# Two weight units loaded and split ahead of the first batch, with the head of an adaLN transformer block reordered

## The reference

```python
mod = (_silu(c) @ wmod).reshape(4, 6, 1, 256)           # sa, ca, ga, sb, cb, gb
h = _layernorm(x) * (1 + ca) + sa                        # x: (4, 512, 256)
x = x + ga * attention(h)                                # 16 heads of 16, causal
h = _layernorm(x) * (1 + cb) + sb
x = x + gb * (shared_ffn(h) + top1_of_8_experts(h))      # inner size 512
```

## Time and profile before

| | |
|---|---|
| median of 3 runs | 450.55 us (447.5 to 451.66) |
| the profiled execution | 449.91 us, of which 448.2 us span |
| granted TensorE clock, mean | 0.983 of full speed |
| PE / DVE / ACT / POOL busy | 89 / 70 / 51 / 48% of the span |
| head (to the first unit of transposed scores) | 0 to 51.2 us |
| block of batch 0 | 51.2 to 105.3 us |

### The profile page before, as it was taken

How to read it: one execution, slowest core, us unless ns; L and a number is a source line. 1 busy time by engine, 2 the same in 40 slices (tenths; PEclk the granted TensorE clock), 3 DMA queues, 4 the chain that set the end, 5 groups by cost and what they waited for, 6 DMA issues and landing times.

```text
span 448.2 us, 8602 instructions
## 1 busy us (share of the span) xinstructions
PE 398.8 (89%) x3009; PEld 225.9 (50%) x3009; DVE 315.2 (70%) x635; ACT 227.8 (51%) x408; POOL 213.1 (48%) x251
## 2 busy tenths in 40 slices
PE   3989987999998997969988799999989999999991
PEld 3344544345453463524444355575566666666660
DVE  7788598689989898699959854979734344443441
ACT  2626557886667865367865655362313332333320
POOL 4755955542376824475536743101602655546242
PEclk9989999999999999899999899999999999999997
DMA  8665499669835599343347014991811344343210
GB/s 272 188 153 118 169 230 252 202 226 308 239 104 174 156 272 283 126 129 114 98 148 231 1 48 173 395 352 66 226 58 26 79 81 96 68 83 70 27 21 0
DMA packets 46192, 67.96 MB, mean 152 GB/s; under 512 B 5380, under 2 KB 33668, under 8 KB 46152
## 3 DMA queue, kind: packets, MB, share of 16 engines
q1 hardware_dynamic: 31064, 36.74, 28.3%
q10 hardware_dynamic: 9936, 22.55, 15.1%
q0 software_dynamic: 5152, 8.14, 9.3%
HBM read 43.14 MB, written 25.18 MB: 152 GB/s over the span
## 4 chain that ended last, share of the span: by engine, by line
PE 60%; DVE 21%; ACT 7%; issue 4%; DMA 3%; POOL 3%; ACTq 1%; SPq 0%; DVEq 0%; POOLq 0%
PE bank L1521 38%; DVE mx L1153 6%; PE bank L1677 4%; PE bank L1661 4%; PE bank L1632 2%; DVE rowg L1254 2%; PE bank L1901 2%; ACT W L903 2%; PE bank L1609 2%; DVE W L1254 1%; DVE x_sb L1198 1%; PE bank L1536 1%; DMA stage<-in_wmod 1%; PE bank L1602 1%; PE bank L1859 1%
## 5 line engine op out<-in xcount | busy, mean ns | idle before, releaser
L903 ACT ACTIVATE W<-bank 128x512 f32<-128x512 f32 (+1 forms) x176 | 93.6, 561 | 55.1 <-PE bank L1661 36.8
L1153 DVE TENSOR_REDUCE mx<-bank 128x1 f32<-128x384 f32 (+3 forms) x176 | 104.7, 632 | 18.4 <-PE bank L1634 15.7
L1521 PE MATMUL bank<-W 128*128 128x256 f16 (+2 forms) x756 | 104.2, 290 | 4.5 <-DVE x_sb L1198 1.8
L1521 PEld LDWEIGHTS bank<-W 128*128 128x128 f16 x756 | 72.8, 99 | 37.4 <-issue 7.3
L770 POOL TENSOR_SCALAR_AFFINE_SELECT W<-W 128x512 f32<-128x512 f32 x64 | 47.9, 749 | 81.8 <-ACT W L903 81.8
L1661 PE MATMUL bank<-W 128*128 128x512 f16 (+3 forms) x256 | 63.2, 304 | 12.1 <-ACT W L903 10.1
L1521 PE MATMUL bank<-W,h2T 128*128 x276 | 67.1, 380 | 0.8 <-issue 0.8
L846 POOL DMA_INDIRECT out<-h2T,sidx x23 | 36.3, 1578 | 63.9 <-DVE h2T L1491 63.5
L1632 PE MATMUL bank<-W 126*128 126x128 f16 (+3 forms) x208 | 52.5, 303 | 5.3 <-DVE mx L1153 4.5
L1677 PE MATMUL bank<-W 128*32 128x128 f32 (+3 forms) x512 | 48.5, 453 | 0.8 <-POOL W L770 0.8
L1661 PEld LDWEIGHTS bank<-W 128*128 128x128 f16 x256 | 21.3, 98 | 48.7 <-ACT W L903 29.5
(11 more groups left out here) (172 smaller groups left out, 562.8 us busy)
## 6 DMA issues: line engine op xcount, KB each, us to landing
w_d<-rowg ACTq DMA_DIRECT2D x18, 512.0 KB, 3.8
W<-w_d SPq DMA_DIRECT2D x18, 512.0 KB, 8.1
stage<-in_gup ACTq DMA_DIRECT2D x14, 512.0 KB
qk_d<-W SPq DMA_DIRECT2D x48, 128.0 KB
W<-qk_d SPq DMA_DIRECT2D x32, 192.0 KB, 5.4
stage<-in_down ACTq DMA_DIRECT2D x7, 512.0 KB
x_sb<-in_x SPq DMA_DIRECT2D x4, 512.0 KB, 8.9
h_d<-gbb SPq DMA_DIRECT2D x4, 512.0 KB, 4.6
```

Source lines behind the costliest of these rows:

```text
L903: a.activation(PT[j][:, i:i + m, :], t_bank(N)[:, 0:m * w].rearrange("p (i n) -> p i n", i=m), ACT.Exp).then_inc(s_exp, 1)
L1153: v.tensor_reduce(mx_v[:, b % 2, hp0 // 4, par, i:i + m, t], s_bank(N)[:, 0:m * w].rearrange("p (i n) -> p i n", i=m), AX.X, ALU.max).then ...
L1521: i = t_.matmul(outp, l, r, start=(n == 0), stop=(n == len(prods) - 1), **kw)
```

## The change

Five edits. **1.** `wmod` is laid out by column blocks, one block in each slot of `stage`, so that slot k comes free with the k-th product that reads it. **2.** SP starts the loads of the units 0 and 1 ahead of its first `qk_out`, and that of unit 2 ahead of the first `maxima_out`. **3.** The units 0 and 1 are split in the head (ACT at n = 14 and 17, DVE at n = 39 and 42) and moved at the steps 1 and 3 of block 0; the other units of block 0 are spread over its steps anew, 6 in place of 8. **4.** `norm1(1)` goes from DVE to ACT, as one activation with a scale and a bias; POOL makes the bias (`shift1`, two small operations). **5.** `stats1(1)` goes from before the head's maxima to n = 17, and the first "v" from n = 13 to n = 11.

```diff
@@ -98,20 +98,33 @@
-          0: {6: 0, 12: 1, 18: 2, 23: 3, 28: 4, 33: 5, 38: 6, 43: 7},
+          0: {6: 2, 13: 3, 20: 4, 26: 5, 33: 6, 40: 7},
...
+HIGHS1, LOWS1, MOVES1 = {14: 0, 17: 1}, {39: 0, 42: 1}, {45: 0, 47: 1}
...
+def low_at(n):
+
+    return LOWS1[n + BU] if n + BU in LOWS1 else splits_at(n - LOWS)
+
+
+def moved_at(n):
+
+    return MOVES1[n + BU] if n + BU in MOVES1 else splits_at(n - MOVES)
...
-HEAD = [(13, "v", 0, 0), (17, "v", 0, 1), (24, "turn", 1, 0), (24, "turn", 1, 1), (20, "mod", 0, 1),
+HEAD = [(11, "v", 0, 0), (17, "v", 0, 1), (24, "turn", 1, 0), (24, "turn", 1, 1), (20, "mod", 0, 1),
@@ -273,7 +287,7 @@
-        wm = stage[:, :, :].rearrange("p a b -> p (a b)").rearrange("p (k n) -> p k n", k=KC)
+        wm = [stage[:, c].rearrange("p (k n) -> p k n", k=KC) for c in range(3)]
@@ -577,7 +592,9 @@
             def stage_load(k):
                 if k == 0:
-                    sp.wait_ge(s_mp, 2)
+                    sp.wait_ge(s_mc, 1)
+                else:
+                    sp.wait_ge(s_mp, k)
                 unit_in(sp, k)
@@ -591,19 +608,19 @@
+            stage_load(0)
+            stage_load(1)
             qk_out(0, 0)
             stacks(0, 0)
             qk_out(0, 1)
             stacks(0, 1)
+            stage_load(2)
             maxima_out(0, 0)
             maxima(0, 0)
-            stage_load(0)
-            stage_load(1)
             qk_out(1, 0)
...
             stacks(1, 0)
-            stage_load(2)
@@ -717,6 +734,13 @@
+            def shift1(b):
+
+                c = slice(TT * b, TT * (b + 1))
+                po.wait_ge(s_rstd, b + 1)
+                link(g.tensor_tensor(mr1[:, :], mv1[:, c, 0], rs1[:, c], ALU.mult))
+                g.tensor_scalar(mr1[:, :], mr1[:, :], -1.0, 0.0, ALU.mult, ALU.add).then_inc(s_shift, 1)
@@ -794,9 +818,10 @@
-            rstd(ve1, mv1, rs1, 1, s_mv, s_rstd)
             qk_low(0, 2)
             qk_low(0, 3)
+            rstd(ve1, mv1, rs1, 1, s_mv, s_rstd)
+            shift1(1)
@@ -893,6 +918,16 @@
+            def norm1(b):
+
+                ac.wait_ge(s_rstd, b + 1)
+                ac.wait_ge(s_shift, 1)
+                ac.wait_ge(s_xt, KC * b)
+                for t in range(TT):
+                    n = TT * b + t
+                    a.activation(xn[:, t], x_sb[:, n], ACT.Identity, bias=mr1[:, t:t + 1],
+                                 scale=rs1[:, n:n + 1]).then_inc(s_xn, 1)
@@ -996,6 +1031,7 @@
             query_parity(1)
+            norm1(1)
@@ -1024,9 +1060,11 @@
+                    if b < 0 and n in HIGHS1:
+                        split_high(HIGHS1[n])
                     if n in SPLITS[b]:
                         split_high(SPLITS[b][n])
-                    moved = splits_at(BU * b + n - MOVES)
+                    moved = moved_at(BU * b + n)
@@ -1328,7 +1366,6 @@
-            stats1(1)
@@ -1336,8 +1373,8 @@
-                    if b < 0 and n == 19:
-                        norm1(1)
+                    if b < 0 and n == 17:
+                        stats1(1)
@@ -1371,7 +1408,7 @@
-                    low = splits_at(BU * b + n - LOWS)
+                    low = low_at(BU * b + n)
```

More of the change, by code:

```diff
@@ L197, in build @@
         rs1 = sb("rs1", [P, NT])
+        mr1 = sb("mr1", [P, TT])
         st2 = sb("st2", [P, NT, 6])
@@ L338, in build @@
         s_rstd = sem("s_rstd")
+        s_shift = sem("s_shift")
         s_xn = sem("s_xn")
@@ L520, in _ @@
             wmod_v = wmod.rearrange("(k p) n -> p k n", p=P)
-            sp.dma_start(wm[:, :, 0:2 * H], wmod_v[:, :, 0:2 * H]).then_inc(s_wm, 16)
+            sp.dma_start(wm[0], wmod_v[:, :, 0:2 * H]).then_inc(s_wm, 16)
             sp.dma_start(bqk[:, :], bqkc).then_inc(s_bqk, 16)
             sp.dma_start(wq_s, wqkvT.rearrange("(k p) n -> p k n", p=P)).then_inc(s_wq, 16)
-            sp.dma_start(wm[:, :, 2 * H:4 * H], wmod_v[:, :, 2 * H:4 * H]).then_inc(s_wmr[0], 16)
-            sp.dma_start(wm[:, :, 4 * H:6 * H], wmod_v[:, :, 4 * H:6 * H]).then_inc(s_wmr[1], 16)
+            sp.dma_start(wm[1], wmod_v[:, :, 2 * H:4 * H]).then_inc(s_wmr[0], 16)
+            sp.dma_start(wm[2], wmod_v[:, :, 4 * H:6 * H]).then_inc(s_wmr[1], 16)
             sp.dma_start(bvb, bqkv[2 * H:3 * H].partition_broadcast(P)).then_inc(s_bias, 16)
@@ L1528, in modulation_columns @@
                     for k in range(KC):
-                        i = t_.matmul(T2[:, 4 * c:4 * c + 4], wm[:, k, P * c:P * (c + 1)], cs[:, 1, k],
+                        i = t_.matmul(T2[:, 4 * c:4 * c + 4], wm[0][:, k, P * c:P * (c + 1)], cs[:, 1, k],
                                       start=(k == 0), stop=(k == KC - 1))
@@ L1535, in modulation_rows @@
                 for k in range(KC):
-                    i = t_.matmul(side_bank("mod", 0, c)[0:B, :], cs[:, 1, k], wm[:, k, 512 * (c + 1):512 * (c + 2)],
+                    i = t_.matmul(side_bank("mod", 0, c)[0:B, :], cs[:, 1, k], wm[c + 1][:, k],
                                   start=(k == 0), stop=(k == KC - 1))
```

## The result

| | median | runs |
|---|---|---|
| before | 449.16 us (447.5 to 451.66) | 4 |
| changed | 453.76 us (451.85 to 455.07) | 4 |

The ratio is 1.0096, with a 95% interval from 1.0056 to 1.0137: 4.3 us slower, where 2.2 us faster was forecast. The profiled execution took 454.18 us, of which 452.4 us span.

What follows compares the result with a forecast made beforehand. Bound taken as PE in most of the head, ACT and PE to 56 us, DVE to 68.5, PE from 77 to 105. 2.0 - 0.3 - 0.1 + 0.3 + 0.3 = 2.2 us off 450.55: 448.4 us, range 445.3 to 451.3.

Steps and rivals of the forecast that it cites:

- The head: Ahead of block 0: without PE's 1.91 us pause behind the first scores, a gain of 2.0 us, bounds 1.2 and 2.2.
- Low halves in the head: Two DVE low halves before block 0: free on DVE, may slow POOL; cost 0.3 us, bounds 0 and 1.6.
- Start of block 0: Moves behind exponentials 1 and 3 may leave ACT idle: cost 0.1 us, bounds 0 and 0.8.
- The keys: Keys of batch 1 through memory, 51 to 63 us: no term in the sum; delay counted only in the slower rival.
- slower rival: Moves 0 and 1 delay batch 1's keys 5.6 us: 452.3 us, chance 0.09; decides from a delay of some 4.5 us.
- signs of being wrong: ACT at modulation rows after 36, PE's key wait at step eleven over 3 us, or 105 us gain not kept.
- Rest of block 0: Fewer, wider-spaced high and low halves shrink PE's later waits: gain 0.3 us, bounds a loss of 0.7, a gain of 1.7.
- The wait of 0.71 at 99.95: PE's wait for ACT in block 0, from a move at step 37 and high half at 38; it goes.
- The 0.98 at 85.12: PE's wait for ACT, from the high half at step 23 with the projections; it moves to the next units.
- The trip of the maxima: Negated maxima through memory before step 22: earlier traffic shortens PE's 0.80 us wait; gain 0.3 us, at most 1.5.
- What is won or lost by 105 us reaches the end: Behind 105 us nothing is tied to a fixed time, so what is won by then should reach the end whole.

Runs made afterwards that it cites:

- e2: Changed kernel with the transfers of moves 0 and 1 cut to one partition each, all places in the lists kept; ratio 0.9956 to the kernel before.
- e5: Changed kernel with only the stores of moves 0 and 1 cut to one partition, their loads whole; ratio 1.0005 to the kernel before.
- e6: Changed kernel with only the loads of units 3 and 4 cut to one partition, the stores whole; ratio 0.9987 to the kernel before.
- e7: e4 with the high halves of block 0 at steps 18, 21, 30, 35, 40, 43; ratio 0.9975 to the kernel before.
- e9: Changed kernel with the low halves of units 2 to 7 cut to 128x64; ratio 1.0057 to the kernel before.
- e4: Changed kernel with moves 0 and 1 back at steps 10 and 16, units 2 to 7 respaced; ratio 0.9957 to the kernel before.
- e10: Kernel before with the low halves of units 2 to 7 cut to 128x64; ratio 0.9971 to the kernel before uncut.

## Why the prediction was wrong

**The head (2.0, measured 1.44).** The mechanism was right at each row: pause gone, the "v" at 1.48 us, the clock at 1.00 behind it, `norm1` on ACT from 31.20 (forecast 30.8), `h_parts` from 35.56 (35.4). The pair of `shift1` took 0.2 us each, less than the 0.6 for both; the four activations took 2.08 and not 1.71. Of the 1.93 us at the group behind the second "v" 0.5 went by 42 us; 0.20 of it is PE waiting at 35.70 for ACT's copy, the place that the prediction named. The size was off by 0.6, inside its bounds.

**Low halves in the head (-0.3).** They did slow POOL: two low halves of its projections (L775) took 3.25 us where they took 2.27, and the last of the keys left at 49.77 behind them. e2 has the same low halves in the head and PE waits 0.69 us for the keys, so without the bytes it costs nothing; what it adds to the wait beside them wasn't measured apart.

**Start of block 0 (-0.1).** Right: ACT idled 0.67 us, PE 0.17.

**The keys (0, measured -4.8).** This is the step that failed. The prediction wrote of its slower rival "1.8 us remain, and these are covered", and left the keys out of the sum; the chance was 0.09. One of its own signs of being wrong, a wait of PE for keys by more than 3 us, is what came (5.18). The traffic was counted against the whole ten microseconds from 50 to 60 and found to fit. But the keys don't use the mean of ten microseconds: they pass through twice, the last piece out from 50.4 to 57.0 and back from 58.9 to 66.5, while transfers were busy 0.89 of the time from 51 to 55 and 1.00 from 55 to 60, and e5 and e6 show that half of the bytes already cost 1.6 to 1.8 us. The rival's own working was good: "5.6 us late", a loss of 4 us in all, and 452.3 us, 1.5 below the measured 453.76. It was given "a delay of some 4.5 us on" as its condition; 4.8 was measured. What was held against it, that reads and writes are spread over all queues, did not keep the keys clear of the moves. By the Trainium skill (DMA: Bandwidth & Descriptors, "Issuing engines are not separate DMA queues") transfers started by different engines interleave on the same 16 DMA engines. The runs agree: ACT's moves made the wait for SP's keys 5.18 and not 0.69 us. The prediction quoted this rule and then gave it too little weight, as no row of the kernel before showed it.

**Rest of block 0 (+0.3, measured -1.26 between steps 22 and 44).** The wait of 0.71 at 99.95 went as forecast. The 0.98 at 85.12 was read wrongly: the prediction gave it to the high half at step 23, but 0.97 remains at the same unit with that high half at 26, and with it at 21 in e7, and 0.67 came at the unit behind. What cost most is the wait of 1.56 for POOL. The prediction priced the spread of high halves on ACT alone; the low half follows two steps later on DVE, and one came to lie on POOL's residual bias (e9). The loss passed the bound of "a loss of 0.7" by 0.56 us, and what the bound left out is the 0.98 us that POOL lost, a price that the row of 1.42 for 0.64 had already shown, and that the prediction used for the head only.

**The trip of the maxima (+0.3).** It did get shorter: issue to issue 2.1 us (72.13 to 74.22) where it was 3.5, and the 0.80 of the earlier trace rows is gone; transfers were busy 0.67 of the time from 66 to 72, before 0.80. Between the keys and step 22 the pauses of PE that its timeline lists fell from 3.0 to 0.5 us. But the rest of that stretch took 12.4 us at the lower clock, where e2, with the same list and the clock at 1.00, took 10.5. In all 0.87 us of the keys' loss came back: 3.37 us late at the keys, 2.50 at step 22. The lower clock, some 1.9 us, stood nowhere in the prediction's sum.

**What is won or lost by 105 us reaches the end.** Right, with 122 in place of 105.

**The sum by measured points:** 1.44 (head) - 4.8 (keys) + 0.9 (from the keys to step 22) - 1.3 (steps 22 to 44) - 0.3 (from there to the issue at 125.77, not looked into) = -4.1 us, against a loss of 4.3 by the ratio.

## What to carry to other kernels

A transfer that is off the critical path can still slow one that is on it, in these runs most where it left ahead of it: before moving bulk traffic, list each round trip through memory in the stretch that it is moved to, and price each one at its own time and not against the free share of a wide window. When a side job is moved, every engine's part of it moves too, and the part that hurts may be on an engine that the move wasn't about. Work that was brought forward need not be shipped forward: with the loads and splits early and the moves at their old place the same change was worth 0.4 to 0.7%.

## What the runs showed of the hardware

**POOL and DVE.** With a low half of DVE beside it (two inputs in SBUF), POOL's two 128x512 operations took 3.25 for 2.27 us and its four 128x256 ones 3.76 for 2.78: about 1 us each time, not far from the length of DVE's operation (1.2 us), which itself grew to 1.30 and 1.60. By the Trainium skill (GPSIMD Engine Reference, "Key points") POOL contends with VectorE instructions that have two SBUF inputs. The traces agree, by these numbers; with the DVE operation cut short in e9 the 3.76 us became 2.79. The place of the low half decides it in other profiles too: 3.77 us in e2 and 3.76 in e7, where one lies on these operations, 2.77 in e4, where none does.

**The clock after a wait.** A standstill of 5.2 us was followed by a granted clock of 0.50 for the next 6 us, and the same products took 0.61 and not 0.40 us. In e5 and e6, with waits of 2.25 and 2.52 us at the same place, the clock stayed at 1.00 and the products took 0.40. By the comparison with e2 above the long wait cost some 1.9 us beyond its length, an estimate.

**The time after 232 us varies.** From the issue of `ng_d` near 232 us to the end, the profiles of the kernel before and the changed one take 216.0 and 216.2 us, and those of the experiments 218.7 to 224.3, whatever was changed ahead. In e10 (the kernel before in that stretch) DVE waits 3.33 us at 319.61, which it doesn't in the first profile; what makes it wait wasn't looked into. So the spans of two profiles can differ by some 8 us for a reason that lies behind the change; points of time ahead of that stretch, and ratios over many runs, are what to compare.
